# Router products as four column groups ahead of the second projection, their sum behind it

## The reference

```python
x = _layernorm(x + attn(x, ...))
x = _layernorm(x + xattn(x, ctx, ctx, ...))
# ffn, on flat = x as (4096, 512)
logits = flat @ router_w.T                               # (4096, 16)
scores = softmax(logits)
_, topk_idx = top_k(logits + router_bias, 2)
topk_scores = take_along_axis(scores, topk_idx); topk_scores /= topk_scores.sum(-1)
out = sum over e of combine[:, e] * (silu(flat @ Wu[e]) * (flat @ Wg[e])) @ Wd[e]
out = out + silu(flat @ Su) * (flat @ Sg) @ Sd
x = _layernorm(x + out)
```

## Time and profile before

| | before |
|---|---|
| median of 3 runs | 2015.57 us (2010.05 to 2018.85) |
| profiled execution | 2011.49 us, its span 2009.9 us |
| mean granted TensorE clock | 0.962 |
| PE busy | 1834.2 us (91%) |
| DVE, POOL, ACT busy | 1141.7, 690.4, 644.1 us |
| the chain that ended last | PE 78%, DVE 11%, issue 4%, ACT 3% |

### The profile page before, as it was taken

One profiled execution on the slowest core, in us unless ns is written; L12 is line 12 of the kernel. 1 busy time (PEld: TensorE's weight loads), 2 busy tenths in 40 slices (PEclk: granted clock), 3 DMA queues, 4 the chain that ended last, 5 costly groups with the idle time before them and its releaser, 6 DMA issues.

```text
span 2009.9 us, 35358 instructions
## 1 busy us (share of the span) xinstructions
PE 1834.2 (91%) x10992; PEld 1175.2 (58%) x10993; DVE 1141.7 (57%) x2407; ACT 644.1 (32%) x1355; POOL 690.4 (34%) x752
## 2 busy tenths in 40 slices
PE   5779999999999999999999999999789999999990
PEld 3456575766757676675766657576444544444440
DVE  3457776777677677766767677676432222222225
ACT  0242433424234252433434233352312211221124
POOL 3214233342323424233343323322224444444440
PEclk7889999999999999999999999998899999999995
DMA  5644243443424344242444424332416577656549
GB/s 160 190 112 113 58 109 83 102 118 69 123 63 102 103 94 127 49 123 74 98 112 89 123 63 102 90 79 73 147 43 134 109 202 168 120 119 145 92 76 342
DMA packets 151420, 225.94 MB, mean 112 GB/s; under 512 B 31888, under 2 KB 106640, under 8 KB 148816
## 3 DMA queue, kind: packets, MB, share of 16 engines
q1 hardware_dynamic: 102048, 132.94, 25.3%
q0 software_dynamic: 38112, 91.86, 20.2%
q10 hardware_dynamic: 11216, 0.61, 0.4%
HBM read 94.44 MB, written 48.57 MB: 71 GB/s over the span
## 4 chain that ended last, share of the span: by engine, by line
PE 78%; DVE 11%; issue 4%; ACT 3%; DMA 2%; SPq 1%; POOL 1%; DVEq 0%; ACTq 0%; POOLq 0%
PE ps L1621 14%; PE ps L1174 11%; PE ps L1111 8%; PE ps L1640 7%; PE ps L1401 6%; PE ps L1376 5%; PE ps L1260 5%; PE ps L1296 3%; PE ps L1365 3%; PE ps L1243 3%; DVE arden L912 3%; DVE smax L894 3%; PE ps L1126 2%; PE ps L1222 2%; PE ps L1609 2%
## 5 line engine op out<-in xcount | busy, mean ns | idle before, releaser
L1621 PE MATMUL ps<-ug_w,rowsT 128*128 x632 | 289.2, 601 | 7.9 <-SPq L1470 4.5
L502 POOL DMA_INDIRECT routed_ids<-pair_w,pos_w x64 | 64.0, 1000 | 446.3 <-DVE pair_w L790 431.7
L1621 PEld LDWEIGHTS ps<-ug_w,rowsT 128*128 128x128 f32 x632 | 121.4, 193 | 161.7 <-issue 161.7
L1510 POOL DMA_INDIRECT sum_rows<-y_sb,pairs x79 | 125.7, 1591 | 245.4 <-DVE y_sb L1588 126.6
L1111 PE MATMUL ps<-wqkv_sb,xT_sb 128*128 128x256 f32 (+1 forms) x512 | 172.6, 491 | 5.8 <-DMA wqkv_sb<-in_wqkv 5.8
L912 DVE RECIPROCAL arden<-ps 128x256 f32<-128x256 f32 x64 | 112.4, 1757 | 114.2 <-PE ps L1365 111.0
L1576 DVE SCALAR_TENSOR_TENSOR silu<-tanh,ps 128x256 f32<-128x256 f32 x79 | 33.2, 421 | 249.4 <-ACT tanh L1531 249.4
L1004 DVE SCALAR_TENSOR_TENSOR weighted<-ps,decay 128x384 f32<-128x384 f32 x256 | 140.2, 553 | 60.7 <-PE ps L1243 51.5
L894 DVE TENSOR_REDUCE smax<-ps 128x2 f32<-128x512 f32 x256 | 163.6, 680 | 13.4 <-PE ps L1296 13.4
L647 ACT ACTIVATE decay<-ps,g_col 128x256 f32<-128x256 f32 x256 | 121.3, 474 | 136.5 <-PE ps L1224 98.9
L1531 ACT ACTIVATE tanh<-ps 128x256 f32<-128x256 f32 x79 | 30.3, 384 | 370.7 <-PE ps L1621 370.7
(11 more groups left out here) (253 smaller groups left out, 3600.2 us busy)
## 6 DMA issues: line engine op xcount, KB each, us to landing
q_stack<-qkT_hi SPq DMA_DIRECT2D x128, 128.0 KB, 3.7
mk_stack<-ctxT_hi SPq DMA_DIRECT2D x128, 128.0 KB
mq_stack<-qkT_hi SPq DMA_DIRECT2D x128, 128.0 KB, 2.4
ug_w<-in_expert_ug SPq DMA_DIRECT2D x16, 1024.0 KB, 5.9
xT_sb<-in_xT SPq DMA_DIRECT2D x16, 512.0 KB, 3.4
q_stack<-qkT_lo SPq DMA_DIRECT2D x64, 128.0 KB, 4.9
x_sb<-in_x POOLq DMA_DIRECT2D x16, 512.0 KB, 3.9
ctxT_sb<-in_ctxT POOLq DMA_DIRECT2D x16, 512.0 KB, 3.8
```

What stands on the lines that cost most here:

```text
L1621: ins = nc.tensor.matmul(ps[:, 2 + k % 2, :], rowsT[:, k % 2, c, :], ug_w[:, bass.ds(slot, 1), c, :].rearrange("p o n -> p (o n)"), start= ...
```

## The change

`rw_sb` is widened from 16 to 32 columns per chunk, cleared by POOL ahead of the load, and the weights go to its first 16 columns. Ahead of the second projection PE issues `route_chunks()`: it waits for `x2T_done` and makes four products, one for each chunk of 128 of the 512 features, with the padded weights (32 columns) as the stationary operand and all 256 tokens of x2T as the moving one; chunk c goes to partitions 32c to 32c + 31 of bank 4. ACT copies the 128x256 result to SBUF (`lgT_sb`, which is the tile `arden`), between the copy x1T_hi and `pass_through(1)`. Behind the second projection `route()` makes two products: the copy's 128 tokens as stationary operand, and `chunk_sum`, a [128, 16] matrix with ones where a row belongs to expert e, as the moving one. That sums the four chunks and turns the result to tokens by experts. DVE reads it in columns 256 to 287 of bank 4. `chunk_sum` is made once, by a DVE reduction over the identity; some counts of semaphores in the prologue grow by one.

```diff
@@ buffers
-        rw_sb = sb("rw_sb", [P, KC, E])
+        rw_sb = sb("rw_sb", [P, KC, HD])
+        chunk_sum = sb("chunk_sum", [P, E])
+        lgT_sb = arden
@@ SP
-            late = [(rw_sb[:, :, :], router_w), (rb_sb[:, :], router_b.partition_broadcast(P)),
+            late = [(rw_sb[:, :, 0:E], router_w), (rb_sb[:, :], router_b.partition_broadcast(P)),
-            sp.wait_ge(consts.sem, 1)
+            sp.wait_ge(consts.sem, 2)
@@ POOL
             nc.gpsimd.memset(gb_sb[:, :], 0.0).then_inc(consts.sem, 1)
+            nc.gpsimd.memset(rw_sb[:, :, :], 0.0).then_inc(consts.sem, 1)
@@ ACT, behind the copy x1T_hi
+                if w is not None:
+                    wait(act, lgT_ready, w, 1)
+                    nc.scalar.copy(lgT_sb[:, :], ps[:, 4, 0:S]).then_inc(lgT_done.sem, 1)
                 if b is not None:
                     pass_through(1)
@@ DVE, prologue and front()
+            nc.vector.tensor_reduce(chunk_sum[:, :], id_sb[:, :].rearrange("p (j n) -> p n j", n=HD)[:, 0:E, :], AX.X, ALU.add)\
+                .then_inc(gwlo.sem, 1)
-                        lg = ps[:, 4, 0:ST * E].rearrange("p (t e) -> p t e", e=E)
+                        lg = ps[:, 4, S:S + ST * E].rearrange("p (t e) -> p t e", e=E)
@@ PE
+                def route_chunks():
+                    wait(pe, x2T_done, w, 1)
+                    for c in range(KC):
+                        ins = nc.tensor.matmul(ps[HD * c:HD * c + HD, 4, 0:S], rw_sb[:, c, :], x2T[:, c, :], start=True, stop=True)
+                    ins.then_inc(lgT_ready.sem, 1)
+
                 def route():
-                    wait(pe, x2T_done, w, 1)
+                    wait(pe, lgT_done, w, 1)
                     for t in range(ST):
-                        for c in range(KC):
-                            ins = nc.tensor.matmul(ps[:, 4, E * t:E * t + E], x2T[:, c, P * t:P * t + P], rw_sb[:, c, :],
-                                                   start=c == 0, stop=c == KC - 1)
+                        ins = nc.tensor.matmul(ps[:, 4, S + E * t:S + E * t + E], lgT_sb[:, P * t:P * t + P], chunk_sum[:, :],
+                                               start=True, stop=True)
                     ins.then_inc(lg_ready.sem, 1)
@@ PE, order of the turn
                 if y is not None:
                     wait(pe, x1_done, y, ST)
                     turn(x1T_ready, x1, 6)
+                if w is not None:
+                    route_chunks()
                 if b is not None:
                     if w is not None:
                         wait(pe, base_done, w, 0)
```

More of the change, by code:

```diff
@@ L307, in attention_and_mlstm @@
         lg_ready, lg_done = sig("lg_ready", 1), sig("lg_done", 1)
+        lgT_ready, lgT_done = sig("lgT_ready", 1), sig("lgT_done", 1)
         top_step, choice_done = sig("top_step", 5 + TOPK), sig("choice_done", 1)
@@ L699, in _ @@
             nc.vector.tensor_scalar(filled[:, :], iota_sb[:, 0:E], float(N), None, ALU.mult).then_inc(gwlo.sem, 1)
-            dve.wait_ge(gwlo.sem, 7)
+            dve.wait_ge(gwlo.sem, 8)
             nc.vector.tensor_scalar(row_p[:, :], row_p[:, :], -1.0, float(P - 1), ALU.mult, ALU.add).then_inc(gwlo.sem, 1)
             nc.vector.tensor_scalar(lo_sign[:, :], is_lo[:, :], 2.0, -1.0, ALU.mult, ALU.add).then_inc(gwlo.sem, 1)
-            dve.wait_ge(gwlo.sem, 9)
+            dve.wait_ge(gwlo.sem, 10)
             for t in range(ST):
                 nc.vector.tensor_scalar(token_f[:, t:t + 1], row_p[:, :], float(P * t), None, ALU.add).then_inc(gwlo.sem, 1)
-            dve.wait_ge(gwlo.sem, 11)
+            dve.wait_ge(gwlo.sem, 12)
             dve.wait_ge(pro.sem, 2 + GQ)
@@ L1119, in gate_mm @@
                     if w is None:
-                        pe.wait_ge(gwlo.sem, 12)
+                        pe.wait_ge(gwlo.sem, 13)
                         pe.wait_ge(late_in.sem, 6 * 16)
@@ L1199, in body @@
                         pe.wait_ge(first_in.sem, 11 * 16)
-                        pe.wait_ge(consts.sem, 3)
+                        pe.wait_ge(consts.sem, 4)
                     turn_qk()
```

## The result

| | before | after |
|---|---|---|
| median | 2016.89 us (4 runs, 2010.05 to 2018.85) | 2081.68 us (4 runs, 2061.53 to 2082.46) |
| ratio to before | | 1.030 (95%: 1.024 to 1.037) |
| profiled execution, span | 2011.49, 2009.9 | 2082.32, 2080.8 |
| mean granted clock | 0.962 | 0.946 |

The account below looks back on a forecast made before the run. PE, busy 91% of the span, was taken as full, with no slack in the side chain at `ug(2)`. 2011.5 + 34.7 (14 x 2.48) - 2 + 18.4 = 2062.6, plus 1.4 offset: forecast 2064 us, eight in ten 2030 to 2078.

Parts of the forecast that it names:

- The wait on x2T and the groups: Ahead of the second projection, PE waits 0.40 for ACT's x2T copy and column groups take 0.55: projection 0.95 late.
- The saving: In `route`, two products replace eight: 0.43 for 1.71, saving 1.28, so PE reaches the gate products 0.33 earlier.
- The hold: DVE's one-hots, issued during POOL's ctxT_hi and ctxT_lo, stand until these end: L957 3.07 later, each turn 2.48 longer.
- the upper end of the step: In the hold on DVE, the cast L942 is held too, about 0.3 more, so 2.8.
- rival 2: In DVE's row only L957 is held: L597 1.57 late, idle 1.9, total 2031.5; chance 0.17.
- the rule for two SBUF inputs: On DVE, an operation with two SBUF inputs is shut out for the whole of a POOL instruction that reads SBUF.
- `ug(2)`: Shared expert's line on PE behind `rank`: starts at 539.46, a turn 2.48 longer, PE standing 2.8 ahead of it.
- The sum without the clock: Whole kernel with the hold but no clock fall (rival 1): 2011.5 + 34.7 - 2 = 2044; chance 0.15.
- The clock: Behind PE's idle 2.8, a fall costs 1.70 to 1.80 in three turns of four: 18.4, ends 0 and 24.5.
- 3 (not slower): DVE gets through beside POOL, L957 ends at 530.66, each turn 0.17 shorter: 2007; chance 0.11.
- 4: Column groups on PE run one after another: projection 2.3 late, L597 3.8 late, total 2087; chance 0.04.

Follow-up runs that it names:

- filled: Changed kernel with twelve unused identity products on PE between `rank` and `ug(2)` in the turns with b and y: 2045.87 us, ratio 1.017 to the kernel before.

## Why the prediction was right and where it was wrong

Times within a turn are counted from the first transpose, 516.97 of before (the timeline's row of L1134) and 533.35 of after.

- **The wait on x2T and the groups:** PE free at 535.10 (the 1.75 from the first transpose to the next line in before), groups from 535.49, projection from 536.06. 0.39 and 0.57, forecast 0.40 and 0.55. Right.
- **The saving:** the two products take 0.37 (541.32 to 541.69), forecast 0.43. `ug(0)` starts 11.15 into the turn in place of 11.46, 0.31 earlier; forecast 0.33. Right. The projection itself became 0.10 longer than the 5.16 of before, which I had not priced; with the wait alone it is 0.11 longer too, so the groups are not the reason.
- **The hold:** the one-hots are held to the end of POOL's second instruction, L966 ends 3.3 later than L957 did, forecast 3.07, and the copy of q and k starts 2.61 later, forecast 2.48. The difference is the cast L951, for which I had kept the upper end of the step: it is held too. The Trainium skill ("SBUF — State Buffer", Who interferes with whom) states that casts can enter a mode that contends with GpSimd, and two-input operations contend with GpSimd's reads; the trace agrees, with 0.86 for 0.17 and 2.65 for 0.49. My price by rows alone with only L957 held (1.57, rival 2) is out. In the prediction I called L957 and L958 both witnesses of the rule for two SBUF inputs; L958 has one such input, so its 2.43 shows a hold but not that rule.
- **`ug(2)`:** 22.58 into the turn in place of 20.01, so 2.57 late; forecast 2.48. Idle 2.91; forecast 2.8.
- **The sum without the clock** was 2044; filled, the kernel takes 2045.9.
- **The clock:** this is the step that failed. "A fall costs 1.70 to 1.80", and three turns in four had one, gave 18.4, at most 24.5. Measured are 31 to 36. The chance of a fall was about right (12 of 14 turns in the profiled execution), its size was not: ten of them lasted 6.8. The trace of after has the price turn by turn, from one first transpose to the next: 89.3 with no fall (260.90 to 350.16), 90.9 with one of 3.4 (350.16 to 441.11), 92.2 with one of 6.8 (533.35 to 625.57). So a fall of 3.4 costs the 1.7 that I had taken, and one of 6.8 costs 2.9, with its first 0.9 lying in the idle stretch; ten of these and two short ones make about 32. In the earlier trace rows the idle stretches ran to 2.61, and the falls behind them lasted 3.4. I took the longer idle here as a reason for more falls and not for longer ones, and so the upper end of 24.5 was no bound at all. The same trace has a longer fall that I left out of the price, 10.2 us that begin in an idle 4.83, in the turn without b (rows below). With 32 to 36 in its place the sum is 2076 to 2080. That nearly every fall was a long one belongs to this execution and those like it: on the later occasion the same program and the same stretches had two long ones, and the clock there cost about 17 us by the medians.
- **The other rivals:** 3 (not slower) decided at L957's end ahead of 530.5; the first one-hot never got that far. 4 fell with the 0.57.

The longer fall of before, the row behind the idle stretch and then a window of it (PE, PEld, DVE, ACT, POOL busy; PEclk, DMA share, GB/s):

```profile
1384.00 1.97 PE L1134 MATMUL ps<-id_sb,x 128*128 128x128 f32 x8 [4.83 <-DVE x L920]
...
1382.60:1392.40 9.80, 8.40 (x40) 8.40 (x41) 4.45 (x15) 1.01 (x1) 4.26 (x7) 0.50 0.19 43
```

The run of after that took 2061.53 had a granted clock of 0.955 against 0.943 to 0.946 in the others. It has no trace of its own, but it is the same program at a higher clock: the price of the clock is not fixed, and a range has to allow for that.

## What to carry to other kernels

When a step is moved, write down the new start of everything on *each* engine and look for pairs that now overlap: here one row moved 1.0 later and another 0.3 earlier, and operations of 0.2 us paid 2.6 us a turn. Work on DVE and POOL that is off the path today may be so only because it happens to lie ahead of the other engine's long instruction; an explicit order between the two (POOL waits for DVE's last urgent step) cost nothing and removed the cliff. A wait on PE must be priced with the clock behind it: the same stretch of 2.9 cost between nothing and 2.9 us on top, so the range has to run from no fall to the longest fall that any trace at hand shows, in every turn.

## What the runs showed of the hardware that was not expected

- A cast of 128x4 elements is held by a POOL cast as the large operations are (0.86 for 0.17), and 0.02 us of issue order decide between 0.19 and 1.06 us for the same operation.
- Twelve idle stretches of 2.9 us on PE in one trace were followed by 6.8 us at 1.2 GHz ten times, by 3.4 once and by none once; twelve of the same length in another by 6.8 twice, by 3.4 seven times, by none three times. Fourteen of 0.9 to 1.5 at the same place were followed by no fall; one of 1.15 elsewhere, close behind another, was.
- On two of the chips the kernel before itself took 2074 to 2076 us, and so all comparisons there are within the chip. In the run with the wait on x2T PE waited 1.1 to 2.5 us at L1347 for ACT's exp of the scores in thirteen turns, where the profile of before has 0.33 at most, and the clock fell behind ten of these waits (0.948 over the whole run); the other traces of these chips show the same. What delays ACT there was not found; it was no part of any edit.
